# A selective-scan block with experts on one core: GpSimd takes over the copy of the scan states at the half of a row

## The chip, the cores and the metric

One core of a Trainium2 chip runs the whole program. The metric is the device time of one execution in microseconds (us). PE is TensorE, DVE is VectorE, ACT is ScalarE, POOL is GpSimd and SP is SyncE; PEld is TensorE's loading of weights.

## The reference

The input is 4 images of 32 x 32 positions with 384 channels, float32. A Mamba-like block comes first and a block of 8 experts, one for each token, second; both are added to their input. Cut to what matters here:

```
def step(h, inp):                       # selective_scan, 4 directions, 16 states n for each channel
    u_t, d_t, B_t, C_t = inp
    dA = jnp.exp(d_t[..., None] * As)
    h = h * dA + (d_t * u_t)[..., None] * B_t[:, :, None, :]
    y = jnp.einsum('bkcn,bkn->bkc', h, C_t)
    return (h, y)
...
xz = x @ in_proj_w.T; xh, z = split(xz); xc = silu(conv3x3(xh) + conv_b)
xs = [rows, columns, rows reversed, columns reversed] of xc, each 1024 positions
x_dbl = einsum(xs, x_proj_w); dts, Bs, Cs = split(x_dbl); dts = softplus(dts @ dt_projs_w + dt_projs_b)
y = sum over the 4 directions of selective_scan(...); y = layernorm(y) * silu(z); out = y @ out_proj_w.T
...
x = x + conv_block(layernorm(x)); t = x + experts(layernorm(x))      # top 1 of 8 experts
```

The recurrence over the 1024 positions is the part that the change touches. Each of the 16 states n is a scan of its own; y is the sum over n of the scan's result times C.

## The kernel before

The program handles two images at a time (a pair, `p`): the 192 channels of two images fill 3 tiles of 128 partitions (`CG = 3`). After projection, convolution and step sizes comes the scan stage, which lies at 172 to 728 us of the span for the first pair and at 971 to 1527 us for the second.

**How the scan stage is cut.** A row of 1024 positions is scanned in two halves of 512. There are 4 directions, in each of them the first half for all 16 states and then the second half for all 16 states: 8 groups of 16 steps, 128 steps for each pair. In this text a first group is one that does the first half of a direction, and a second group one that does the second half. `place(s)` gives for a step the direction, the group, the half, the state n and whether the group is a first one. A second group starts each scan from the state with which the first one ended; that is kept in `state[:, n, 0:3]`, one number for each of the 3 tiles of a partition.

**What a step is.** (1) Its input, du times B, is made by GpSimd (n = 0, 4, 8, 12), by VectorE (odd n up to 13) or by ScalarE and TensorE together (n = 2, 6, 10, 14, 15), as the letters P, D and A of `MAKER` say. (2) ScalarE makes the decay exp(delta times A), 3 instructions (`exp`, L683 into PSUM, or L678 into SBUF for the letter A), in a ring of two PSUM banks. (3) VectorE does 3 scans (`scans`, L916), in place, in one of the 7 ring slots `X3`. (4) In a first group the state is copied: column 511 of each of the 3 tiles, or column 0 where the direction runs backwards. (5) GpSimd multiplies the slot by C in place, one instruction of 128 x 1536 (L472), and counts `s_hc`. (6) TensorE adds the slot up in PSUM (`add_up`, L1203) and frees it (`s_xfree`).

**The order on each engine.** It is written out by hand. GpSimd: the input for step s + 2 where that is its own (`input_of`, L457), then waits for C and for the 3 scans of step s, in first groups also for `s_state`, then the product (L472). ScalarE: the first two exponentials of step s + 1, then `keep_state(s)` (L692), then the rest; the second of these exponentials waits for the third scan of step s. TensorE: in step s the transposes of an input of the letter A (`transpose_input`, L1229), then `add_up` of step s - 2; `transpose_du` (L1216) follows step 13. Since TensorE takes these in order, the scan of an A step s waits for the transposes, and these wait behind the add-up of step s - 3, which needs GpSimd's product of step s - 3. VectorE: the input for step s + 1 where it is its own (L892), then the 3 scans of step s. SyncE loads rows of B and C (L344), each when its ring slot is free; for C that is `s_hc`.

Of the kernel before, what the change touches and what calls it, by code (L numbers as in the profile page):

```python
# [9 lines left out]
ALU = mybir.AluOpType  # L10
ACT = mybir.ActivationFunctionType
# [7 lines left out]
CG = 3  # L19
KC = DM // P  # L20
TT = L // P
HALF = 512
# [7 lines left out]
RING, B_RING, C_RING = 7, 4, 6  # L30
# [9 lines left out]
KORDER = (0, 2, 1, 3)  # L40
# [9 lines left out]
def build(nc, x, w_in, conv_w, conv_b, w_xd, w_dt, bias_row, a_log, d_skip, ln_g, ln_b, w_out,  # L50
          w_gate, b_gate, w1, w2, w3, sel, ident_d, half_ones, tri_d, out):
    ctx = ExitStack()
    with ctx:
# [17 lines left out]
        ones = sb("ones", [P, P])  # L71
# [33 lines left out]
        X3 = [carve(CG * HALF).rearrange("p (j l) -> p j l", j=CG) for _ in range(IN_ARENA)]  # L105
# [25 lines left out]
        state = carve(NS * CG).rearrange("p (n j) -> p n j", n=NS)  # L131
# [144 lines left out]
        STEPS = ND * 2 * NS  # L276

        def place(s):

            kk, first = s // (2 * NS), (s // NS) % 2 == 0  # L280
            return kk, s // NS, int(first == (KORDER[kk] >= 2)), s % NS, first
# [8 lines left out]
        def states_before(c):  # L290
            return c // (2 * NS) * NS + min(c % (2 * NS), NS)
# [131 lines left out]
        @block.gpsimd  # L423
        def _(g):
            g.memset(padf, 0.0).then_inc(s_pad, 1)
            g.memset(ones[:, :], 1.0).then_inc(s_setup, 1)
            g.sem_inc(s_gap, 4)
            g.iota(lane[:, :], [[0, 1]], base=1, channel_multiplier=1, allow_small_or_imprecise_dtypes=True)\
             .then_inc(s_iota, 1)
            for p in range(PAIRS):  # L430
                if p:
                    g.wait_ge(s_xfree, STEPS * p)
                    g.memset(padf, 0.0).then_inc(s_pad, 1)

                for t in range(1, 9):
                    g.wait_ge(s_prod, 9 * p + t + 1)
                    if t > 1:
                        g.wait_ge(s_taps, 8 * p + t - 1)
                    g.tensor_tensor(acc3[:, BY_POOL, :], acc3[:, BY_POOL, :], tap[t % 2], ALU.add).then_inc(s_taps, 1)  # L439
                for i, kk in enumerate(PREP):  # L440
                    if i >= 2:
                        g.wait_ge(s_dust[i % 2], 16 * (2 * p + 1))
                    for j in range(CG):
                        n, d = CG * (ND * p + i) + j + 1, delta3[i % 2][:, j, :]
                        g.wait_ge(s_delta, n)
                        g.tensor_tensor(du3[i % 2][:, j, :], d, (xc3 if kk < 2 else xcT3)[:, j, :], ALU.mult)\  # L446
                         .then_inc(s_du, 1)
                def input_of(s):

                    _, gr, _, n, _ = place(s)  # L450
                    c = STEPS * p + s
                    g.wait_ge(s_steps[gr % 2], 32 * (GROUPS_OF_PAIR // 2 * p + gr // 2 + 1))
                    r = rows_before(c)
                    g.wait_ge(s_b[r % B_RING], 32 * (r // B_RING + 1))
                    if c >= RING:
                        g.wait_ge(s_xfree, c - RING + 1)
                    g.tensor_tensor(X3[c % RING], steps[gr % 2][1], Bs[r % B_RING][:, None, :].to_broadcast([P, CG, HALF]),  # L457
                                    ALU.mult).then_inc(s_dbp, 1)

                for s in range(STEPS):  # L460
                    kk, _, _, n, first = place(s)
                    c = STEPS * p + s
                    if s == 0:
                        input_of(0)
                    if s + 2 < STEPS and MAKER[(s + 2) % NS] == "P":
                        input_of(s + 2)
                    g.wait_ge(s_c[c % C_RING], 32 * (c // C_RING + 1))
                    g.wait_ge(s_scan, CG * (c + 1))
                    if first:
                        g.wait_ge(s_state, states_before(c + 1))  # L470
                    x = X3[c % RING]
                    g.tensor_tensor(x, x, Cs[c % C_RING][:, None, :].to_broadcast([P, CG, HALF]), ALU.mult)\  # L472
                     .then_inc(s_hc, 1)
                g.wait_ge(s_zld, 16 * (p + 1))
                for h in range(2):
                    cs = slice(h * HALF, (h + 1) * HALF)
                    g.wait_ge(s_yg, 2 * CG * p + CG * h + 1)
                    for b in range(2):
                        src = slice(64 * b, 64 * b + 64)
                        ins = g.tensor_tensor(yz3[0:64, b, cs], y3[src, 0, cs], g3(z2)[src, 0, cs], ALU.mult)  # L480
                    ins.then_inc(s_yzp, 1)

            g.wait_ge(s_ops, 16 * PAIRS)
            small_ok = dict(allow_small_or_imprecise_dtypes=True)
            g.iota(iota_n, [[1, NT]], base=0, channel_multiplier=0, **small_ok).then_inc(s_iota, 1)
            g.iota(rev, [[-1, NE]], base=NE, channel_multiplier=0, **small_ok).then_inc(s_iota, 1)
            g.iota(iota_m, [[1, P]], base=0, channel_multiplier=0, **small_ok).then_inc(s_iota, 1)
            g.iota(block_no, [[2 * TT, PAIRS], [1, TT], [TT, 2]], base=0, channel_multiplier=0, **small_ok)\
             .then_inc(s_iota, 1)

            g.wait_ge(s_iota, 5)
            g.wait_ge(s_tile, 1)
            g.tensor_tensor(number_of[:, :, 0, :], in_tile, block_no[:, :, None].to_broadcast([P, TILES, NT]),
                            ALU.mult).then_inc(s_num, 1)

            g.wait_ge(s_tst, 16 * 2 * GROUPS * PAIRS)
            g.wait_ge(s_first, 1)

            def load_rows(k, rows):
                g.indirect_dma_start(xs[k], None, t_dram, bass.IndirectOffsetOnAxis(rows, 0)).then_inc(s_xs[k], 16)  # L500

            for k in range(4):
                load_rows(k, first_rows[:, k:k + 1])

            def store_rows(n, k, more):

                g.wait_ge(s_gap, n + 1)
                g.wait_ge(s_yo, n + 1)
                g.tensor_tensor(gap[:, k:k + 1], one[:, :], one[:, :], ALU.mult).then_inc(s_gap, 1)  # L509

                g.indirect_dma_start(out, bass.IndirectOffsetOnAxis(move[:, k, 0:1], 0), yo[k % 2], None,
                                     bounds_check=TOK - 1, oob_is_err=False).then_inc(s_yst[k % 2], 16)
                if more:
                    load_rows(k, move[:, k, 1:2])

            with g.Fori(0, NT // 4 - 1) as i:
                for w in range(4):
                    store_rows(i * 4 + w, w, True)
            for w in range(4):
                store_rows(NT - 4 + w, w, False)  # L520
            for u in range(2):
                g.wait_ge(s_yst[u], 16 * (NT // 2))
# [3 lines left out]
        def _(a):  # L526
# [13 lines left out]
            for p in range(PAIRS):  # L540
# [142 lines left out]
                    a.activation(dA[e % 2], steps[g % 2][0][:, j, :], ACT.Exp,  # L683
                                 scale=A[:, KORDER[kk], j, n:n + 1]).then_inc(s_dA, 1)

                def keep_state(s):

                    kk, _, _, n, _ = place(s)
                    c = STEPS * p + s
                    at = 0 if KORDER[kk] >= 2 else HALF - 1  # L690
                    a.wait_ge(s_scan, CG * (c + 1))
                    a.activation(state[:, n, :], X3[c % RING][:, :, at], ACT.Copy).then_inc(s_state, 1)  # L692

                def y_out(g):

                    kk, _, half, _, _ = place(g * NS)
# [12 lines left out]
                for s in range(STEPS):  # L709
                    kk, g, _, n, first = place(s)  # L710
                    todo = [(g * NS + m if m > n else (g + 1) * NS + m, f, l) for m, f, l in SCALED.get(n, ())]
                    exp(s, 0)
                    exp(s, 1)
                    if s == 0:
                        duT_out(0)
                        du_to_psum(0)
                        scale_duT(BY_SCALAR[0], 0, 3)
                    if s and place(s - 1)[4]:
                        keep_state(s - 1)
                    if MAKER[n] == "A" or n % 2:  # L720
                        exp(s, 2)
                    if n == NS - 1 and g + 1 < GROUPS_OF_PAIR:
                        du_to_psum(g + 1)
                    for m, f, l in todo:
                        if m < STEPS:
                            scale_duT(m, f, l)
                    if n == 2 and g:
                        y_out(g - 1)
                    if not (MAKER[n] == "A" or n % 2):
                        exp(s, 2)  # L730
                    if n == NS - 2 and g + 1 < GROUPS_OF_PAIR:
                        duT_out(g + 1)
# [730 lines left out]
```

## Time and profile before

| | us |
|---|---|
| median of 3 runs | 1968.33 (1968.18 to 1974.79) |
| the profiled execution, its own time | 1967.72 |
| its span in the trace | 1965.9 |
| scan stages in it, 2 x about 555 | about 1111 |
| mean granted TensorE clock | 0.908 |

The page gives each engine's busy time over the whole span; as the stages have different limits, the scan stages are read by themselves, with views restricted to stretches of time. The waits give idle time of an engine and what ended it. The timeline gives instructions in order of time, equal neighbours merged ("x4"), with the idle time before them in brackets.

### The profile page before, as it was taken

The page shows a single profiled execution, that of the slowest core. Times are in us where ns is not written, and L with a number is a line of the kernel's source. Part 1 is how long each engine was busy: PE and PEld are TensorE (multiplying, and loading weights), DVE is VectorE, ACT ScalarE, POOL GpSimd, SP SyncE. Part 2 cuts the span into 40 slices and gives each one's busy share as a digit, 9 for nine tenths or more (in the row PEclk, how much of TensorE's full clock was granted, in tenths as well). Part 3 has the DMA queues.
Part 4 walks back from the last instruction along what each step waited for, and adds up shares of the span by engine and source line. Part 5 has one row for each costly group of instructions (what it writes and reads, how often), then busy time and mean ns, then how long its engine had stood idle before and what let it go on. Part 6 is the DMA issues. An engine that isn't in the chain of part 4 may idle for free.

```text
span 1965.9 us, 17747 instructions
## 1 busy us (share of the span) xinstructions
PE 1569.6 (80%) x5004; PEld 781.3 (40%) x5005; DVE 1467.5 (75%) x1586; ACT 1073.5 (55%) x1944; POOL 1306.9 (66%) x501
## 2 busy tenths in 40 slices
PE   5765788788888875977488878877888668999997
PEld 2222334334433432622134433433443244555554
DVE  5468999999999977455799999999999572332222
ACT  3557767777777752364677777876776211111110
POOL 1337999999999981042599999999999112222221
PEclk9876999999999997787599899999998878999999
DMA  3147345344434331212834434433432481111110
GB/s 115 43 174 247 102 130 177 97 134 149 128 105 139 102 120 67 73 38 91 310 104 138 149 112 139 134 107 130 136 100 70 181 310 38 45 48 45 51 49 14
DMA packets 107360, 228.15 MB, mean 116 GB/s; under 512 B 18302, under 2 KB 31137, under 8 KB 103440
## 3 DMA queue, kind: packets, MB, share of 16 engines
q1 hardware_dynamic: 102160, 213.02, 32.7%
q0 software_dynamic: 5120, 14.21, 2.3%
q8 instruction: 33, 0.54, 0.1%
q14 instruction: 47, 0.39, 0.1%
HBM read 184.13 MB, written 44.60 MB: 116 GB/s over the span
## 4 chain that ended last, share of the span: by engine, by line
PE 44%; DVE 21%; POOL 18%; issue 12%; ACT 4%; DMA 1%; DVEq 0%; POOLq 0%; SPq 0%; ACTq 0%
POOL arena L472 15%; DVE arena L916 13%; PE psum L1203 11%; PE psum L1341 10%; PE psum L1360 5%; PE psum L1136 3%; PE psum L1152 3%; POOL arena L457 2%; DVE arena L892 2%; PE psum L1229 2%; PE psum L1177 2%; PE psum L1269 1%; PE psum L1216 1%; PE psum L1288 1%; DVE arena L872 1%
## 5 line engine op out<-in xcount | busy, mean ns | idle before, releaser
L472 POOL TENSOR_TENSOR arena<-arena 128x1536 f32<-128x1536 f32 x256 | 877.6, 3449 | 30.9 <-ACT arena L692 16.9
L1203 PE MATMUL psum<-arena,ident 128*128 128x512 f32 x1536 | 717.7, 619 | 70.6 <-POOL arena L472 70.4
L916 DVE TENSOR_TENSOR_SCAN arena<-psum,arena 128x512 f32<-128x512 f32 x528 | 614.6, 1228 | 0.1
L683 ACT ACTIVATE psum<-arena 128x512 f32<-128x512 f32 x528 | 363.4, 690 | 259.4 <-DVE arena L916 249.3
L1203 PEld LDWEIGHTS psum<-arena,ident 128*128 128x128 f32 x1536 | 295.7, 199 | 457.0 <-issue 325.9
L916 DVE TENSOR_TENSOR_SCAN arena<-arena,psum 128x512 f32<-128x512 f32 x240 | 282.5, 1231 | 37.2 <-PE psum L1229 34.0
L1229 PE MATMUL psum<-ident,arena 128*128 128x128 f32 x960 | 154.4, 295 | 143.0 <-DVE arena L916 142.8
L660 ACT ACTIVATE arena<-arena 128x192 f32<-128x192 f32 x640 | 234.6, 440 | 0.0
L457 POOL TENSOR_TENSOR arena<-arena 128x1536 f32<-128x1536 f32 x64 | 220.4, 3443 | 0.0
L892 DVE TENSOR_TENSOR arena<-psum,arena 128x1536 f32<-128x1536 f32 x112 | 193.8, 1731 | 13.6 <-ACT psum L668 12.2
L1341 PE MATMUL psum<-arena 128*128 x480 | 203.7, 561 | 0.0
L1229 PEld LDWEIGHTS psum<-ident,arena 128*128 128x128 f32 x960 | 112.2, 148 | 201.8 <-DVE arena L916 140.5
L768 ACT ACTIVATE arena<-psum 128x384 f32<-128x384 f32 x40 | 19.6, 490 | 301.6 <-PE psum L1332 301.6
L678 ACT ACTIVATE arena<-arena 128x512 f32<-128x512 f32 x240 | 161.3, 710 | 14.2 <-DVE arena L916 14.1
L446 POOL TENSOR_TENSOR arena<-arena 128x1024 f32<-128x1024 f32 x24 | 60.4, 2517 | 148.1 <-DVE arena L877 148.1
L509 POOL TENSOR_TENSOR gap<-one 128x1 f32<-128x1 f32 x40 | 11.3, 284 | 211.9 <-DVE arena L1078 211.9
L1341 PEld LDWEIGHTS psum<-arena 128*128 128x128 f32 x480 | 88.8, 192 | 77.5 <-issue 67.3
L1061 DVE TENSOR_TENSOR arena<-arena,psum 128x469 f32<-128x469 f32 x40 | 25.7, 643 | 124.1 <-ACT arena L773 114.4
L439 POOL TENSOR_TENSOR arena<-arena 128x1024 f32<-128x1024 f32 x16 | 38.0, 2374 | 114.2 <-ACT arena L572 112.2
L1360 PE MATMUL psum<-arena 128*128 (+1 forms) x320 | 110.0, 487 | 1.0 <-DVE arena L1068 1.0
L1177 PE MATMUL psum<-arena 64*128 64x512 f32 x96 | 63.3, 807 | 24.4 <-DVE arena L877 22.6
L872 DVE SCALAR_TENSOR_TENSOR arena<-arena 128x1024 f32<-128x1024 f32 x24 | 43.5, 1811 | 51.7 <-ACT arena L624 51.6
(161 smaller groups left out, 1480.3 us busy)
## 6 DMA issues: line engine op xcount, KB each, us to landing
arena<-bc_dram SPq DMA_DIRECT2D x864, 128.0 KB, 3.0
step_dram<-arena SPq DMA_DIRECT2D x16, 1536.0 KB, 7.9
arena<-step_dram SPq DMA_DIRECT2D x32, 768.0 KB, 7.7
arena<-in_x SPq DMA_DIRECT2D x8, 1536.0 KB, 10.3
arena<-in_w SPq DMA_DIRECT2D x6, 1876.0 KB, 11.1
t_dram<-arena SPq DMA_DIRECT2D x16, 386.0 KB, 4.4
arena<-in_w SPq DMA_DIRECT2D x4, 1536.0 KB, 14.9
z_dram<-arena SPq DMA_DIRECT2D x2, 1536.0 KB, 5.1
```

Source lines behind the costliest of these rows:

```text
L457: g.tensor_tensor(X3[c % RING], steps[gr % 2][1], Bs[r % B_RING][:, None, :].to_broadcast([P, CG, HALF]), ALU.mult).then_inc(s_dbp, 1)
L472: g.tensor_tensor(x, x, Cs[c % C_RING][:, None, :].to_broadcast([P, CG, HALF]), ALU.mult)\
L660: a.activation(blocks(scaled[index % 2])[:, :, k, b, :], blocks(duT)[:, :, k, b, :], ACT.Copy, scale=BT[:, kk, LB * half + k, b, BY_SCALAR ...
L678: a.activation(dAs[j], steps[g % 2][0][:, j, :], ACT.Exp, scale=A[:, KORDER[kk], j, n:n + 1]).then_inc(s_dAs, 1)
L683: a.activation(dA[e % 2], steps[g % 2][0][:, j, :], ACT.Exp, scale=A[:, KORDER[kk], j, n:n + 1]).then_inc(s_dA, 1)
L892: v.tensor_tensor(X3[c % RING], dups, Bs[r % B_RING][:, None, :].to_broadcast([P, CG, HALF]), ALU.mult).then_inc(s_dbv, 1)
L916: v.tensor_tensor_scan(x, decay, given, 0.0 if first else state[:, n, j:j + 1], ALU.mult, ALU.add).then_inc(s_scan, 1)
L1177: ins = pe.matmul(bank[2 + 2 * j + h], wdt[0:64, KORDER[PREP[i]], j, :], xd[i % 2][0:64, h * HALF:(h + 1) * HALF], start=True, stop=True)
L1203: ins = pe.matmul(bank[j], ident[:, :], X3[c % RING][:, j, :], start=False, stop=(n == NS - 1), skip_group_check=True)
L1229: ins = pe.transpose(dA[e % 2][:, k * P:(k + 1) * P], scaled[index % 2][:, at:at + P], ident[:, :])
L1341: ins = pe.matmul(bk[:, 0:F], xsT[u][:, k, :], w[:, k, bass.ds(e * F, F)], start=(k == 0), stop=(k == KC - 1))
L1360: ins = pe.matmul(bank[6 + u][:, 0:DM], hidT[u][0:m, k, :], W3[0:m, k, bass.ds(e * DM, DM)], start=(k == 0), stop=(k == FC - 1))
```

## The change

In a first group GpSimd copies the state itself, ahead of its product with C; the copy is a multiplication of 128 x 3 numbers (stride 512) by ones. The wait for `s_state`, which was for ScalarE's copy, now is for its own copy. ScalarE's `keep_state`, and its wait for the scans, are gone. There are 16 such copies in each of 4 first groups for 2 pairs, 128 in all.

```diff
@@ -466,9 +466,11 @@
                         input_of(s + 2)
                     g.wait_ge(s_c[c % C_RING], 32 * (c // C_RING + 1))
                     g.wait_ge(s_scan, CG * (c + 1))
+                    x = X3[c % RING]
                     if first:
+                        at = 0 if KORDER[kk] >= 2 else HALF - 1
+                        g.tensor_tensor(state[:, n, :], x[:, :, at], ones[:, 0:CG], ALU.mult).then_inc(s_state, 1)
                         g.wait_ge(s_state, states_before(c + 1))
-                    x = X3[c % RING]
                     g.tensor_tensor(x, x, Cs[c % C_RING][:, None, :].to_broadcast([P, CG, HALF]), ALU.mult)\
                      .then_inc(s_hc, 1)
                 g.wait_ge(s_zld, 16 * (p + 1))
@@ -683,14 +685,6 @@
                     a.activation(dA[e % 2], steps[g % 2][0][:, j, :], ACT.Exp,
                                  scale=A[:, KORDER[kk], j, n:n + 1]).then_inc(s_dA, 1)
 
-                def keep_state(s):
-
-                    kk, _, _, n, _ = place(s)
-                    c = STEPS * p + s
-                    at = 0 if KORDER[kk] >= 2 else HALF - 1
-                    a.wait_ge(s_scan, CG * (c + 1))
-                    a.activation(state[:, n, :], X3[c % RING][:, :, at], ACT.Copy).then_inc(s_state, 1)
-
                 def y_out(g):
 
                     kk, _, half, _, _ = place(g * NS)
@@ -715,8 +709,6 @@
                         duT_out(0)
                         du_to_psum(0)
                         scale_duT(BY_SCALAR[0], 0, 3)
-                    if s and place(s - 1)[4]:
-                        keep_state(s - 1)
                     if MAKER[n] == "A" or n % 2:
                         exp(s, 2)
                     if n == NS - 1 and g + 1 < GROUPS_OF_PAIR:
```

## Rows read from the trace of the kernel before

**Rows 1.** The page, part 1: busy time, share of the span and instructions of each engine.
```profile
PE 1569.6 (80%) x5004; PEld 781.3 (40%) x5005; DVE 1467.5 (75%) x1586; ACT 1073.5 (55%) x1944; POOL 1306.9 (66%) x501
```

**Rows 2.** Two groups: stretch, PE, PEld, DVE, ACT, POOL busy, PEclk, DMA share, GB/s.
```profile
172.50:241.10 68.60, 50.26 (x158) 25.24 (x159) 65.32 (x56) 50.23 (x106) 64.12 (x19) 0.90 0.34 112
241.10:310.80 69.70, 57.22 (x173) 27.75 (x172) 68.46 (x57) 50.79 (x94) 68.48 (x21) 0.95 0.39 125
```

**Rows 3.** Timeline of POOL, first direction and first group of the second.
```profile
176.92 6.84 POOL L472 TENSOR_TENSOR arena<-arena 128x1536 f32<-128x1536 f32 x2 [6.43 <-ACT arena L692]
...
187.11 13.65 POOL L472 TENSOR_TENSOR arena<-arena 128x1536 f32<-128x1536 f32 x4
200.71 3.44 POOL L457 TENSOR_TENSOR arena<-arena 128x1536 f32<-128x1536 f32 x1
204.11 13.74 POOL L472 TENSOR_TENSOR arena<-arena 128x1536 f32<-128x1536 f32 x4
...
221.20 13.63 POOL L472 TENSOR_TENSOR arena<-arena 128x1536 f32<-128x1536 f32 x4
...
262.32 6.97 POOL L472 TENSOR_TENSOR arena<-arena 128x1536 f32<-128x1536 f32 x2 [0.25 <-DVE arena L916]
...
315.25 6.88 POOL L472 TENSOR_TENSOR arena<-arena 128x1536 f32<-128x1536 f32 x2 [0.70 <-ACT arena L692]
...
350.18 6.86 POOL L472 TENSOR_TENSOR arena<-arena 128x1536 f32<-128x1536 f32 x2 [0.82 <-ACT arena L692]
```

**Rows 4.** Timeline of all engines, the turn from first to second group.
```profile
223.24 6.78 DVE L916 TENSOR_TENSOR_SCAN arena<-psum,arena 128x512 f32<-128x512 f32 x6
...
228.07 2.84 PE L1203 MATMUL psum<-arena,ident 128*128 128x512 f32 x6 [0.55 <-POOL arena L472]
...
232.06 1.04 PE L1229 MATMUL psum<-ident,arena 128*128 128x128 f32 x8
...
232.80 6.78 DVE L916 TENSOR_TENSOR_SCAN arena<-arena,psum 128x512 f32<-128x512 f32 x6 [2.78 <-PE psum L1229]
```

**Rows 5.** Timeline of DVE, second group of the first direction.
```profile
241.14 7.15 DVE L916 TENSOR_TENSOR_SCAN arena<-psum,arena 128x512 f32<-128x512 f32 x6
...
258.56 7.15 DVE L916 TENSOR_TENSOR_SCAN arena<-psum,arena 128x512 f32<-128x512 f32 x6
...
301.88 7.35 DVE L916 TENSOR_TENSOR_SCAN arena<-arena,psum 128x512 f32<-128x512 f32 x6 [1.13 <-PE psum L1229]
```

**Rows 6.** Waits of POOL, whole span: us in total, times, longest us.
```profile
POOL arena L472 <- ACT arena L692: 16.9, 11, 6.4
POOL arena L472 <- DVE arena L916: 10.8, 30, 0.5
```

**Rows 7.** Waits of DVE in the scans, and of PE for POOL, whole span.
```profile
DVE arena L916 <- PE psum L1229: 34.0, 25, 3.6
DVE arena L916 <- ACT arena L678: 1.9, 2, 1.0
PE psum L1203 <- POOL arena L472: 70.4, 56, 3.1
```

**Rows 8.** Timeline of ACT at the start of the second direction; groups by line for L692.
```profile
314.27 0.69 ACT L683 ACTIVATE psum<-arena 128x512 f32<-128x512 f32 x1 [0.42 <-DVE arena L916]
314.89 0.19 ACT L692 ACTIVATE arena<-arena 128x3 f32<-128x3 f32 x1
...
L692 ACT ACTIVATE arena<-arena 128x3 f32<-128x3 f32 x128 | 24.9, 195 | 9.8 <-DVE arena L916 9.8
```

**Rows 9.** Instructions of a line on POOL: duration ns min/median/max; the smallest one by group.
```profile
L509 POOL TENSOR_TENSOR gap<-one x40: 183/287/323, 1645.2 to 1956.0; 128x1 f32<-128x1 f32 x40
L446 POOL TENSOR_TENSOR arena<-arena x24: 2345/2352/3412, 83.9 to 963.2; 128x1024 f32<-128x1024 f32 x24
L472 POOL TENSOR_TENSOR arena<-arena x256: 3417/3448/3479, 176.9 to 1523.5; 128x1536 f32<-128x1536 f32 x128
L439 POOL TENSOR_TENSOR arena<-arena x16: 2351/2380/2385, 43.7 to 858.1; 128x1024 f32<-128x1024 f32 x16
L428 POOL IOTA lane<- 128x1 f32 x1 | 0.1, 127 | 0.0
```

**Rows 10.** Timeline of POOL: eight dependent sums (L439), and the expert stage.
```profile
43.71 20.01 POOL L439 TENSOR_TENSOR arena<-arena 128x1024 f32<-128x1024 f32 x8 [39.67 <-ACT arena L572]
...
1677.73 0.28 POOL L509 TENSOR_TENSOR gap<-one 128x1 f32<-128x1 f32 x1 [5.11 <-DVE arena L1078]
1678.50 1.02 POOL L511 DMA_INDIRECT out<-arena,move  x1 [0.48 <-issue]
```

## The prediction, made before the changed kernel ran

> **What bounds the kernel now.** The busy shares of the page come first, and they mislead: GpSimd is at 66% and VectorE at 75% of the whole span [rows 1]. The change lies in the scan stages alone, so I read those by themselves. Over one direction VectorE is busy for 65.3 of 68.6 us in the first group and 68.5 of 69.7 us in the second; GpSimd for 64.1 us of the first (it can't begin before the first scan is done, at 176.9) and 68.5 us of the second [rows 2]. Both are nearly full, so the question is which of them waits for the other, and where.
>
> GpSimd's timeline answers that. It starts at 176.92 and then runs without a pause through the whole first group; the first idle time is the 0.25 us at 262.32, in the second group. Later first groups have few pauses, the longest of them 0.82 us at 350.18 [rows 3]. Four steps of a first group hold 4 products and one input, 5 instructions of 128 x 1536, and start again after 204.11 - 187.11 = 17.0 us, so one instruction takes a pitch of 3.40 us (less than its recorded 3.448 us [rows 9], since neighbours overlap a little). VectorE's pace in a first group would be 6.78 us for six scans. That VectorE is the faster one there shows at its step 14: it ends its scans at 223.24 + 6.78 = 230.0 and stands still for 2.78 us [rows 4]. What ends that stall, TensorE's transposes of the input, stands in TensorE's order behind the add-up of step 11, and that began at 228.07, when GpSimd's product was done [rows 4]. So in first groups **GpSimd sets the pace**, through TensorE's queue; VectorE waits 34.0 us for these transposes in all, and TensorE 70.4 us for GpSimd [rows 7].
>
> In a second group the six scans take 7.15 us, and four steps 258.56 - 241.14 = 17.42 us [rows 5]. There VectorE is the slower one, by 0.42 us in four steps; GpSimd waits for it in small pieces, 0.25 us at 262.32 for one [rows 3]. Still step 14 of the second group stalls for 1.13 us on the transposes [rows 5], so even there GpSimd is right behind.
>
> How much does GpSimd stand still? The two waits of L472 add up to 16.9 + 10.8 = 27.7 us [rows 6]. Two of them, 6.43 us for the first pair and as much for the second, are the start of a pair, when there is no scan to multiply yet. What is left is 27.7 - 12.9 = 14.8 us in the 8 directions, under 2 us in each. That is all the slack of the engine that gets the new work.
>
> **The change part by part.** (a) *ScalarE loses 128 copies* of 195 ns, 24.9 us busy [rows 8]. ScalarE's exponentials hold up no scan: among VectorE's waits in the scans only 1.9 us is for ScalarE [rows 7], and ScalarE is busy for 50 of 69 us of a group [rows 2]. I take this at nothing; the upper bound of the gain is the 1.9 us.
>
> (b) *GpSimd no longer waits for ScalarE.* This wait can be seen where GpSimd has caught up: at the start of the second direction ScalarE first does an exponential (314.27, 0.69 us), then the copy (314.89, 0.19 us), and GpSimd's product starts at 315.25 [rows 3, 8]. The copy could have started about 0.1 us after the scan, at about 314.3, but GpSimd itself was busy until 314.55. At each pair's start some 0.9 us of the 6.43 us is of this kind (0.69 + 0.19), nearly 2 us for both pairs. In the steps at which GpSimd lags behind, the copy was long done, and nothing is saved.
>
> (c) *GpSimd gets 128 copies, and each is followed by a wait for itself.* The trace has no 128 x 3 product on GpSimd. The nearest row is the 128 x 1 product L509, 287 ns (183 to 323) [rows 9]. A line through 1024 elements in 2.352 us and 1536 in 3.448 us has a slope of 2.14 ns an element and meets zero elements at 0.16 us, so 3 elements would take 0.17 us. The smallest instruction of any kind took 0.127 us [rows 9]. I take 0.25 us, between the line and the 128 x 1 row and nearer to the latter. The wait for its own semaphore also has a row: the eight L439, each of which waits for the one before, cover 20.01 us, with 2.38 us each; 20.01 - 2.38 = 17.63 us for 7 pitches is 2.52 us, so 0.14 us pass between the end of one and the start of the next [rows 9, 10]. Copy and wait: 0.25 + 0.14, about **0.40 us for each**, with bounds of 0.127 + 0.14 = 0.27 us and, from above, 0.77 us, the time from the start of L509 to the start of the instruction behind it (1677.73 to 1678.50), which is an indirect DMA with an issue of its own [rows 10]. Something like 0.6 us is the highest that I give weight. Queued behind the waiting copy on GpSimd are the product of the same step and the input of step s + 4; who waits for them is TensorE's add-up, then VectorE at the next A step, and SyncE with the C row, whose slot is 6 steps deep and hides it.
>
> The Trainium skill bears on this (Perfetto Trace Analysis, GPSIMD Engine Instruction): it says that recorded spans of GpSimd don't compose and that starts should be compared with starts. By recorded span alone a copy is 0.28 us and the sum would be 128 x 0.28 - 15 = +21 us; by the one start-to-start figure there is, 0.77 us, it would be +84 us. The L439 rows agree with the rule: 2.38 us recorded, 2.52 us from start to start.
>
> (d) *What takes up the new work.* 128 x 0.40 = 51 us go onto an engine that is the bound in every first group. Nothing hides a copy there: in the first direction GpSimd has no idle time from its first product to the fifth of the second group. What comes off is the slack. A GpSimd that enters the second group later doesn't meet its small waits for VectorE any more, and waits less at the next direction's start: at most the 14.8 us. In the last group of a pair no new direction follows and VectorE sets the pace to the end, so I take only about 13 us of them. With the 2 us of (b) that is **15 us saved**, bounds 11 and 18 us. The second bound holds if neighbours of a small wait become quicker too (two products took 6.97 us behind such a wait and 6.84 us without [rows 3]).
>
> (e) *Beyond GpSimd.* From the end of product 11 to the start of scan 14 there are 4.7 us (228.07 to 232.80 [rows 4]), three scans take 3.4 us more; GpSimd has three instructions, 10.2 us, and two copies to do before it needs that scan. So the way over TensorE gives GpSimd no new wait, and TensorE's clock, 0.90 and 0.95 in these groups [rows 2], has over 2 us of room.
>
> Sum: 1967.7 + 51 - 15 = 2003.7; the median lies 0.6 us above the profiled execution, so **2004 us**.
>
> **The rivals.** *One, VectorE is the bound and the copies are hidden.* For it: 75% against 66% busy, and GpSimd does wait 30 times for scans. Then the time stays within some 5 us of 1968. Against it: the 2.78 and 1.13 us stalls of VectorE, both behind GpSimd, and a first group in which GpSimd never stands still [rows 3]. *Two, the other side: the removed wait is worth more than the copy.* The point from which it decides is 15 / 128 = 0.12 us for a copy with its wait. If GpSimd took the copy in 0.05 us, the sum would be 6.4 - 15 = -9 us, 1959 us. For it: where GpSimd caught up, it saves an exponential and a copy on ScalarE. Against it: the own wait alone measured 0.14 us. *Three, a dear copy.* A small instruction between two large ones costs what it costs ahead of the DMA, near 0.7 us: 128 x 0.7 - 13 = +77 us, 2045 us. For it: the only start-to-start figure of a small product. Against it: 0.48 us of that stand as issue of the indirect DMA. *Four, a cheap one.* Copy and wait at the lower bounds, 0.27 us: 35 - 17 = +18 us, 1986 us.
>
> **How the numbers follow.** Forecast, 0.32 to 0.5 us for each copy, 1992 to 2019 us: 0.60. Cheap copy, 1979 to 1992: 0.13. Dear, above 2019: 0.16, most of it under 2045. VectorE the bound: 0.08. Gain: 0.03. The range reaches from the cheap copy to 0.6 us for each with 12 us saved (77 - 12 = +65 us): 1984 to 2033. About 0.5%, 10 us, is what a measurement of this kernel can tell from no change. Slower by more: 0.60 + 0.16 + 0.13 less a little of the cheap case, 0.88. Within: 0.09. Faster: 0.03.
>
> **What would show it.** Right: GpSimd's waits in the scans fall from 27.7 us to the start of each pair and little more; the first step of L472 after a copy starts 0.4 us after the copy's start; VectorE's waits for the transposes grow from 34 us to some 70 us and more; each direction takes 4 to 5 us longer, nearly all of it in its first group; nothing changes outside the scan stages. Wrong: GpSimd keeps idle time in second groups, or first groups grow by less than 16 copies; or the copy's start-to-start time isn't near 0.4 us, which scales the sum and nothing else.

## The result: slower by 1.2%, and where the time went

| | us |
|---|---|
| before, median of 4 runs beside it | 1971.34 (1968.18 to 1974.79) |
| changed, median of 4 runs | 1995.69 (1994.41 to 1996.58) |
| ratio | 1.0123, 95% interval 1.0099 to 1.0146 |
| profiled execution: before, changed | 1967.72, 1995.23 |
| its span: before, changed | 1965.9, 1993.4 |

The lines move by 2 to 8: GpSimd's product is L474 now and its copy L472, the scans are L908, the transposes L1221, the add-up L1195. The waits of GpSimd in the changed kernel answer [rows 6]:

```profile
POOL arena L472 <- DVE arena L908: 11.1, 2, 5.6
POOL arena L474 <- DVE arena L908: 6.9, 20, 0.6
```

No wait for ScalarE is left; 27.7 us have become 18.0 us, 11.1 us of them at the two starts of a pair. The waits of VectorE and TensorE answer [rows 7]:

```profile
DVE arena L908 <- PE psum L1221: 60.1, 31, 5.5
PE psum L1195 <- POOL arena L474: 91.1, 55, 4.0
```

VectorE stands still for 60.1 us before its scans and not 34.0, TensorE waits 91.1 us for GpSimd's product and not 70.4. The start of GpSimd's timeline answers [rows 3]:

```profile
176.86 0.19 POOL L472 TENSOR_TENSOR arena<-arena,ones 128x3 f32<-128x3 f32 x1 [5.56 <-DVE arena L908]
177.14 3.44 POOL L474 TENSOR_TENSOR arena<-arena 128x1536 f32<-128x1536 f32 x1
180.53 0.19 POOL L472 TENSOR_TENSOR arena<-arena,ones 128x3 f32<-128x3 f32 x1
180.81 3.44 POOL L474 TENSOR_TENSOR arena<-arena 128x1536 f32<-128x1536 f32 x1
184.20 3.43 POOL L457 TENSOR_TENSOR arena<-arena 128x1536 f32<-128x1536 f32 x1
...
283.50 6.97 POOL L474 TENSOR_TENSOR arena<-arena 128x1536 f32<-128x1536 f32 x2 [0.24 <-DVE arena L908]
```

From the copy's start to the product's start 0.28 us pass, and the product still ends 3.39 us after its start as far as the next instruction is concerned. Nothing overlaps the copy. In this first direction there is no idle time up to 283.50, the ninth product of the second group. At step 14 of the first group, where VectorE stood still for 2.78 us [rows 4], it now stands still for 4.86 us:

```profile
224.91 6.79 DVE L908 TENSOR_TENSOR_SCAN arena<-psum,arena 128x512 f32<-128x512 f32 x6
236.55 6.78 DVE L908 TENSOR_TENSOR_SCAN arena<-arena,psum 128x512 f32<-128x512 f32 x6 [4.86 <-PE psum L1221]
```

**Where the time lies.** VectorE begins each group with an input of its own (L892, now L884), so the starts of these instructions cut the span into groups. In the profiled execution of before the 8 first groups add up to 554.4 us, of the changed kernel to 578.5 us: +24.1 us, 3.0 us for each. The six second groups that have a successor take 417.0 and 416.3 us. The stretch ahead of the first group is 0.8 us longer, the one from the last group of the first pair to the second pair 0.4 us shorter, and all from the last group on 3.7 us longer. 24.1 - 0.7 + 0.8 - 0.4 + 3.7 = 27.5 us, the difference of the two spans. VectorE's instructions didn't get slower: it is busy for 1467.5 us before and 1467.4 us now.

Where one group is taken to end matters a little. Counted on GpSimd, from its first product of a group to its first product of the next, the first groups grow from 549.0 to 579.0 us (30.0 of the 35.5 us that 128 copies of 0.277 us add), and the six second groups shrink from 421.0 to 416.5 us. The table below uses VectorE's count; where GpSimd's says something else, the text gives it.

The 3.7 us at the end lie in the stage between the scans and the experts. The same stretch, from 80 us behind the start of the last group to 332 us before the end, is in before and in the changed kernel (busy time of PE, PEld, DVE, ACT, POOL, then the granted clock):

```profile
1534.60:1633.90 99.30, 60.11 (x281) 37.02 (x282) 64.15 (x138) 22.31 (x36) 16.90 (x13) 0.74 0.59 220
1558.38:1661.40 103.02, 65.55 (x281) 39.57 (x282) 64.38 (x138) 20.89 (x35) 16.90 (x13) 0.70 0.57 212
```

The same 281 matmuls take 60.1 us of TensorE at a mean granted clock of 0.74 and 65.6 us at 0.70. Of the kernels below, e2 and e3 show 0.74 and 0.73 there, e1 and e4 0.69, with no link to the edit that I can see.

### The profile page after: what moved, and what is told of

Read it like the earlier page. It is cut to its first block, busy times and chain, and to the rows that moved or that the text cites. A ratio compares the mean times of both kernels' runs of the same rounds, so it can differ in the third digit from the quotient of the medians.

```text
span 1993.4 us, 17747 instructions
## 1 busy us (share of the span) xinstructions
PE 1583.2 (79%) x5004; PEld 785.6 (39%) x5005; DVE 1467.4 (74%) x1586; ACT 1061.0 (53%) x1816; POOL 1331.1 (67%) x629
## 4 chain that ended last, share of the span: by engine, by line
PE 42%; POOL 20%; DVE 19%; issue 14%; ACT 3%; DMA 1%; DVEq 0%; POOLq 0%; ACTq 0%
POOL arena L474 16%; PE psum L1195 12%; DVE arena L908 10%; PE psum L1333 10%; PE psum L1352 5%; PE psum L1144 3%; POOL arena L457 2%; PE psum L1128 2%; PE psum L1221 2%; PE psum L1169 2%; DVE arena L884 1%; DVE arena L864 1%; POOL arena L439 1%; PE psum L1208 1%; PE psum L1343 1%
## 5 line engine op out<-in xcount | busy, mean ns | idle before, releaser
L474 POOL TENSOR_TENSOR arena<-arena 128x1536 f32<-128x1536 f32 x256 | 880.4, 3450 | 18.8 <-DVE arena L908 6.9
L1195 PE MATMUL psum<-arena,ident 128*128 128x512 f32 x1536 | 729.3, 627 | 91.6 <-POOL arena L474 91.1
L908 DVE TENSOR_TENSOR_SCAN arena<-psum,arena 128x512 f32<-128x512 f32 x528 | 615.1, 1233 | 0.1
L1195 PEld LDWEIGHTS psum<-arena,ident 128*128 128x128 f32 x1536 | 299.3, 201 | 485.8 <-issue 330.9
L908 DVE TENSOR_TENSOR_SCAN arena<-arena,psum 128x512 f32<-128x512 f32 x240 | 281.8, 1233 | 61.1 <-PE psum L1221 60.1
L1221 PE MATMUL psum<-ident,arena 128*128 128x128 f32 x960 | 150.2, 291 | 133.2 <-DVE arena L908 133.2
L884 DVE TENSOR_TENSOR arena<-psum,arena 128x1536 f32<-128x1536 f32 x112 | 194.3, 1735 | 13.0 <-ACT psum L670 12.2
L1221 PEld LDWEIGHTS psum<-ident,arena 128*128 128x128 f32 x960 | 110.3, 145 | 189.9 <-DVE arena L908 129.1
L680 ACT ACTIVATE arena<-arena 128x512 f32<-128x512 f32 x240 | 158.4, 710 | 17.4 <-DVE arena L908 17.4
L439 POOL TENSOR_TENSOR arena<-arena 128x1024 f32<-128x1024 f32 x16 | 38.0, 2377 | 114.4 <-ACT arena L574 112.4
L1169 PE MATMUL psum<-arena 64*128 64x512 f32 x96 | 63.3, 806 | 24.4 <-DVE arena L869 22.6
## 6 DMA issues: line engine op xcount, KB each, us to landing
arena<-in_w SPq DMA_DIRECT2D x4, 1536.0 KB, 12.6
```

The costliest lines, as they stand in the source:

```text
L680: a.activation(dAs[j], steps[g % 2][0][:, j, :], ACT.Exp, scale=A[:, KORDER[kk], j, n:n + 1]).then_inc(s_dAs, 1)
L884: v.tensor_tensor(X3[c % RING], dups, Bs[r % B_RING][:, None, :].to_broadcast([P, CG, HALF]), ALU.mult).then_inc(s_dbv, 1)
L908: v.tensor_tensor_scan(x, decay, given, 0.0 if first else state[:, n, j:j + 1], ALU.mult, ALU.add).then_inc(s_scan, 1)
L1169: ins = pe.matmul(bank[2 + 2 * j + h], wdt[0:64, KORDER[PREP[i]], j, :], xd[i % 2][0:64, h * HALF:(h + 1) * HALF], start=True, stop=True)
L1195: ins = pe.matmul(bank[j], ident[:, :], X3[c % RING][:, j, :], start=False, stop=(n == NS - 1), skip_group_check=True)
L1221: ins = pe.transpose(dA[e % 2][:, k * P:(k + 1) * P], scaled[index % 2][:, at:at + P], ident[:, :])
```

## The experiments

Each kernel ran beside the kernel before on its chip. The medians of the kernel before differ by up to 5.4 us from set to set (1968.3 to 1973.7), so kernels of different sets are best compared by their ratios. The two sums are those of above, from one profiled execution of each kernel: 8 first groups, and 6 second groups. The diffs leave out new tiles and semaphores.

| kernel | median us | ratio to before (95%) | first groups | second groups |
|---|---|---|---|---|
| before | 1968 to 1974 | 1 | 554.4 | 417.0 |
| changed | 1995.69 | 1.0123 (1.0099 to 1.0146) | 578.5 | 416.3 |
| e1 copy twice | 2024.38 | 1.0253 (1.0236 to 1.0270) | 602.2 | 421.3 |
| e2 both copies | 1991.77 | 1.0087 (1.0070 to 1.0104) | 581.8 | 416.4 |
| e3 shorter product | 1958.40 | 0.9917 (0.9900 to 0.9933) | 548.0 | 415.9 |
| e4 ScalarE earlier | 1969.91 | 0.9982 (0.9964 to 1.0001) | 551.4 | 417.9 |
| f1 copy by VectorE | 2039.94 | 1.0344 (1.0317 to 1.0372) | 625.6 | 417.0 |
| f2 bare product | 1990.34 | 1.0093 (1.0066 to 1.0120) | 572.5 | 416.6 |
| f3 copies in second groups | 1995.03 | 1.0117 (1.0088 to 1.0146) | 558.2 | 434.4 |
| f4 an input to VectorE | 1978.92 | 1.0032 (1.0012 to 1.0051) | 562.0 | 422.0 |
| h1 reduction by VectorE | 1976.82 | 1.0022 (1.0003 to 1.0040) | 568.7 | 416.3 |
| h2 changed + f4 | 1985.30 | 1.0063 (1.0041 to 1.0085) | 564.1 | 421.9 |
| h3 e4 + f4 | 1969.14 | 0.9981 (0.9960 to 1.0002) | 551.3 | 422.6 |

**e1, each copy twice.**

```diff
                     if first:
                         at = 0 if KORDER[kk] >= 2 else HALF - 1
+                        g.tensor_tensor(state[:, n, :], x[:, :, at], ones[:, 0:CG], ALU.mult).then_inc(s_twice, 1)
+                        g.wait_ge(s_twice, states_before(c + 1))
                         g.tensor_tensor(state[:, n, :], x[:, :, at], ones[:, 0:CG], ALU.mult).then_inc(s_state, 1)
```

> The changed kernel with each copy done twice, each followed by its own wait (256 copies). A copy takes 0.277 us from its start to the start of the product in the trace of the changed kernel. Theory A (GpSimd's own time sets the pace of the first groups): 128 x 0.277 = 35 us more, less what is left of GpSimd's small waits for scans (6.9 us there, of which at most 5 go): +30 to +35 us over the changed kernel, about 2026 us. Theory B (the time comes from another place, such as one wait in each step that hides a second copy, or VectorE as the bound): under +10 us.

Measured 2024.4 us, +28.7 us over the changed kernel by the medians and +26 us by the ratios: 1 to 4 us under theory A's range, and far from theory B's 10 us. The first groups grew by another 23.7 us and the second ones by 5.0 us (on GpSimd's count by 30.6 and -0.8 us, so a second copy costs there what the first did). The copies stand one behind the other at 0.27 us:

```profile
176.95 0.19 POOL L473 TENSOR_TENSOR arena<-arena,ones 128x3 f32<-128x3 f32 x1 [5.55 <-DVE arena L911]
177.22 0.19 POOL L475 TENSOR_TENSOR arena<-arena,ones 128x3 f32<-128x3 f32 x1
177.49 3.44 POOL L477 TENSOR_TENSOR arena<-arena 128x1536 f32<-128x1536 f32 x1
```

The product's waits for scans shrink from 6.9 us to 1.8 us; what little slack there was is used up.

**e2, ScalarE's copy kept and GpSimd's work added.**

```diff
                     x = X3[c % RING]
+                    if first:
+                        at = 0 if KORDER[kk] >= 2 else HALF - 1
+                        g.tensor_tensor(spare[:, n, :], x[:, :, at], ones[:, 0:CG], ALU.mult).then_inc(s_extra, 1)
+                        extra[0] += 1
+                        g.wait_ge(s_extra, extra[0])
                     g.tensor_tensor(x, x, Cs...
```

> The kernel before, ScalarE's copy kept, and in first groups an extra copy of the same 128 x 3 numbers by GpSimd into a spare tile, with its own wait. It does the second half of the change (GpSimd's work) without the first (ScalarE's copy gone). Theory A: as the changed kernel, plus the 0.87 us at each of the two starts of a pair: +26 to +29 us over before, about 1997 us. Theory B (the change costs because the copy itself now lies on the way of the state): the extra copy is needed by nobody, so clearly less than the changed kernel, under +15 us.

The first groups grew by 27.4 us over before, 3.3 us more than with the change: a copy that nobody needs costs as much as the real one, so it is GpSimd's time and not the way of the state. The time as a whole is a miss: the ratio gives +17 us (14 to 20) over before where +26 to +29 us was expected, close to theory B's bound of 15 us. The kernel before took 1973.7 us beside it; against before's profiled execution, 6 us faster, e2's profiled span is 24.3 us longer. The median is also 4 us under the changed kernel's: all from the last group on took 510.9 us, the changed kernel's 515.1 us, at a granted clock of 0.74 and 0.70 in the stage behind the scans. So theory A rests here on the group sums, where the edit acts, and not on the median.

**e3, a shorter product.** The product leaves out 129 of 1536 elements in first groups.

```diff
-                    g.tensor_tensor(x, x, Cs[c % C_RING][:, None, :].to_broadcast([P, CG, HALF]), ALU.mult)\
+                    w = HALF - 43 if first else HALF
+                    g.tensor_tensor(x[:, :, 0:w], x[:, :, 0:w], Cs[c % C_RING][:, None, 0:w].to_broadcast([P, CG, w]), ALU.mult)\
```

> The changed kernel, but the product with C leaves out the last 43 of 512 columns of each tile in first groups (129 of 1536 elements), so that part of the product is left out. At 2.14 us for 1000 elements that is 0.276 us less for each product, as much as a copy with its wait takes. Theory A: GpSimd's time in a step is that of before, the time goes back to the kernel before or 2 to 6 us under it: 1963 to 1972 us. Theory B (not GpSimd's time in total but the waits around the copy): stays near 1996 us.

1958.4 us, 37 us under the changed kernel. Taking 128 x 0.28 = 36 us off GpSimd gives back all that the copies took, and more than the expected return to before: the first groups are 6.4 us under before, 0.8 us each. From start to start the shorter product takes 3.13 us where the whole one takes 3.40, so GpSimd's time in a step is that of before here, and I read the 6.4 us as what the change gains by not waiting for ScalarE. On GpSimd's count it is 3.2 us in first groups and 3.0 us in second ones. e2, which keeps ScalarE's copy, is 3.3 us over the changed kernel in first groups; e4 shows 3.0 us, not clear of noise. The time is 5 us below the expected range. Theory B is out.

**e4, ScalarE's copy one exponential earlier**, in the kernel before.

```diff
                     exp(s, 0)
+                    if s and place(s - 1)[4]:
+                        keep_state(s - 1)
                     exp(s, 1)
...
-                    if s and place(s - 1)[4]:
-                        keep_state(s - 1)
```

> The kernel before, with ScalarE's copy of the state put between its first and second exponential of the next step, so that it runs when the third scan is done and not one exponential (0.69 us) later. Theory A: only GpSimd's waits for ScalarE shrink, which are 16.9 us in 11 places, 11 of them unavoidable at the two starts of a pair: 0.5 to 0.7 us at most of them, -3 to -6 us against before, 1963 to 1968 us. Rival (the later exponential delays the scans, which wait for it): +5 us or more.

The ratio of 0.9982 (0.9964 to 1.0001) fits -3 to -6 us but isn't clear of no change; the first groups are 3.0 us shorter, the second ones 0.9 us longer, and on GpSimd's count the two sums together are those of before (969.8 and 970.0 us). So a gain isn't shown. The rival, +5 us, is out.

**f1, the copy by VectorE**, behind its scans, with a wait for them; GpSimd's copy is gone.

```diff
                     scans(s)
+                    kk, _, _, n, first = place(s)
+                    if first:
+                        ...
+                        v.wait_ge(s_scan, CG * (c + 1))
+                        v.tensor_copy(state[:, n, :], X3[c % RING][:, :, at]).then_inc(s_state, 1)
```

> The changed kernel with the copy given to VectorE, right behind the three scans of the step and after a wait for them; GpSimd waits for it as it did for ScalarE. Theory A (GpSimd sets the pace of first groups, VectorE has 34 us of waits for TensorE there): VectorE's extra 128 x some 0.2 to 0.3 us go into its own waits, and GpSimd's wait for a state shrinks by some 0.5 us where it has caught up: 0 to -5 us against before. Rival (VectorE is the bound in first groups): 128 x 0.25 = +30 us against before, as much as the change itself.

A clear miss: +69 us, and the first groups 71.2 us longer. VectorE's timeline shows why, with GpSimd's beside it:

```profile
185.77 1.22 DVE L906 TENSOR_TENSOR_SCAN arena<-arena,psum 128x512 f32<-128x512 f32 x1 [0.17 <-PE psum L1225]
187.03 1.70 DVE L918 COPY arena<-arena 128x3 f32<-128x3 f32 x1
188.64 3.44 DVE L906 TENSOR_TENSOR_SCAN arena<-psum,arena 128x512 f32<-128x512 f32 x3
...
226.03 2.07 DVE L918 COPY arena<-arena 128x3 f32<-128x3 f32 x1
```

```profile
185.28 3.42 POOL L457 TENSOR_TENSOR arena<-arena 128x1536 f32<-128x1536 f32 x1
...
224.65 3.43 POOL L457 TENSOR_TENSOR arena<-arena 128x1536 f32<-128x1536 f32 x1
```

The copy of 3 numbers that begins at 187.03 lasts until 188.73; GpSimd's product that was running ends at 188.70. The one at 226.03 ends at 228.10, GpSimd's at 228.08. All copies show it: the 26 that begin while GpSimd is idle take 0.168 to 0.171 us, and each of the 102 that begin while it works ends 0.02 to 0.03 us after GpSimd's running instruction. The 128 copies last 0.168 to 3.43 us, 734 ns in the mean, 93.9 us in all; that is 72 us over 128 x 0.17 us, and the first groups grew by 71.2 us. A copy of VectorE waits until GpSimd's running instruction is through, and the scans behind it wait as well. It is neither theory's mechanism; h1 tests it.

**f2, a small product without its wait**, in first groups of the kernel before.

```diff
+                    if first:
+                        m = states_before(c)
+                        g.tensor_tensor(spare[:, m, :], ones[:, 0:CG], ones[:, CG:2 * CG], ALU.mult)
```

> The kernel before, ScalarE's copy kept, and in first groups an extra product of 128 x 3 ones on GpSimd into a spare tile of its own, with no wait behind it. It measures what a small instruction costs on GpSimd without the wait for itself. In the changed kernel 0.277 us pass from the copy's start to the product's start, 0.199 us of it the recorded copy. Theory A1 (the cost is mostly the instruction): 0.15 to 0.2 us for each from start to start, first groups 8 x 16 x 0.17 - 6 = +12 to +20 us longer than before. A2 (the cost is mostly the wait, small instructions overlap as the start-up fills do at 0.03 us): under +5 us.

```profile
182.38 0.20 POOL L475 TENSOR_TENSOR spare<-ones 128x3 f32<-128x3 f32 x1
182.52 3.43 POOL L476 TENSOR_TENSOR arena<-arena 128x1536 f32<-128x1536 f32 x1
```

0.15 us from start to start (127 of the 128), at a recorded 0.195 us, and the first groups grew by 18.1 us: A1 holds. So of the 0.28 us of the change about 0.15 us are the small instruction and 0.13 us the wait for it. The change itself without that wait wasn't tried: the product overwrites in place what the copy reads, and only the wait orders the two.

**f3, the extra copies of e2 in second groups only** (`if not first`).

> The kernel before with the extra GpSimd copy and its own wait (0.277 us) in second groups only, 128 of them. Theory A with slack: in second groups VectorE is the slower by 0.42 us in four steps and GpSimd waits 1 to 2 us in each; so of 4.4 us for each group 1.5 to 2 us are hidden: +19 to +24 us over before, a little less than in first groups. Rival (VectorE alone sets the pace there): under +8 us.

+23 us by the ratio, and 434.4 - 417.0 = 17.4 us in six second groups, 2.9 us each, of the 16 x 0.28 = 4.4 us that were added; the first groups grew by 3.8 us. Second groups, whose pace VectorE sets by a hair, pay nearly as much as first ones (3.4 us in e2). The slack there is 1.5 us, as expected, and no more.

**f4, one input from GpSimd to VectorE**, in the kernel before; the string has 32 letters now, for a first and a second group, and is indexed by the step modulo 32.

```diff
-MAKER = "PDADPDADPDADPDAA"
+MAKER = "PDADPDADPDADDDAAPDADPDADPDADPDAA"
```

> The kernel before (ScalarE's copy), but in first groups VectorE, not GpSimd, makes the input of n = 12: 3.4 us off GpSimd and 1.65 us onto VectorE in each of 8 first groups. Theory A: VectorE's stall of 2.8 us at step 14 of a first group goes, 1.65 us of it is refilled: -1 to -1.7 us for each first group, -8 to -14 us against before, second groups unchanged. Rival (VectorE is the bound): +13 us.

A miss again: 1978.9 us, 6 us slower than before by the ratio (2 to 10), with first groups 7.6 us longer in sum where I expected 8 to 14 us less. First and second groups together are 12.6 us longer (on either count), nearly the rival's +13 us: VectorE's added time, 8 x 1.65 us, came through almost whole. The 2.78 us stall did shrink to 0.89 us, but GpSimd, with 3.4 us less to do, now stands still before three products in a row:

```profile
220.05 3.44 POOL L472 TENSOR_TENSOR arena<-arena 128x1536 f32<-128x1536 f32 x1 [1.49 <-ACT arena L692]
225.06 3.44 POOL L472 TENSOR_TENSOR arena<-arena 128x1536 f32<-128x1536 f32 x1 [1.57 <-ACT arena L692]
230.06 6.87 POOL L472 TENSOR_TENSOR arena<-arena 128x1536 f32<-128x1536 f32 x2 [1.57 <-ACT arena L692]
```

Its steps last 3.35 + 1.65 = 5.0 us, VectorE's time for three scans and an input. So GpSimd is ahead as the bound by very little: take some work off it and put it on VectorE, and VectorE with the way over ScalarE's copy is the bound at once. The waits for that copy are 64.5 us in 36 places, against 16.9 us in 11.

**h1, the state by a reduction of VectorE** in place of f1's copy.

```diff
-                        v.tensor_copy(state[:, n, :], X3[c % RING][:, :, at]).then_inc(s_state, 1)
+                        v.tensor_reduce(state[:, n, :], X3[c % RING][:, :, at:at + 1], AX_X, ALU.max).then_inc(s_state, 1)
```

> VectorE keeps the state as in f1_vector_copy, but by a reduction (maximum over one element) instead of a copy. In f1 the copies lasted 0.168 to 3.43 us, and the long ones ended when a product of GpSimd ended. Theory C (the copy takes a port that GpSimd's running instruction holds, and the reduction, which reads one input in the plain mode, does not): no long ones, some 0.2 us a step on VectorE, first groups at 68.5 to 69.5 us as before: 1968 to 1978 us. Rival (the wait for its own scan, or any small read of VectorE, is what costs): as f1, 2030 to 2040 us.

```profile
L918 DVE TENSOR_REDUCE arena<-arena x128: 156/158/160, 177.8 to 1469.4; 128x3 f32<-128x3 f32 x128
```

All 128 take 156 to 160 ns, beside f1's 168 to 3430 ns for the same numbers (min, median and max):

```profile
L918 DVE COPY arena<-arena x128: 168/250/3430, 177.9 to 1523.7; 128x3 f32<-128x3 f32 x128
```

The time falls from 2039.9 to 1976.8 us. The first groups, 71.1 us each, miss the expected 68.5 to 69.5 us; the profiled execution took 1987.6 us, 11 us more than the median, and how much of this lies in the groups isn't known. Only the kind of instruction differs from f1, so it is the copy's wait for GpSimd that costs 63 us, and theory C holds in its effect. The Trainium skill (GPSIMD Engine Reference, Key points) says that GpSimd shares its interfaces to SBUF with VectorE and conflicts with VectorE's instructions in a two-port mode or with two SBUF inputs. The two runs agree with a conflict of this kind: 0.158 us for each reduction, up to 3.43 us for a copy. No row names the mode of either instruction, so that the mode is the reason isn't shown.

**h2, the changed kernel with f4's edit.**

> The changed kernel, with the input of n = 12 in first groups made by VectorE instead of GpSimd. Theory A (GpSimd's own time bounds the first groups of the changed kernel: 20 instructions at 3.40 us and 16 copies at 0.277 us = 72.4 us, measured 71.6 to 73.5): 3.4 us come off GpSimd, and VectorE (65.2 + 1.65 us and some stalls) takes over at 68.5 to 69.5 us, -2.5 to -3.5 us for each first group: -20 to -28 us against the changed kernel, 1968 to 1976 us. Rival (something else than GpSimd's time, as the latency of copy and wait): +0 to -8 us against it.

The right sign, half the size: -10 us by the medians, -14.4 us in the first groups (1.8 us each, expected 2.5 to 3.5), +5.6 us in the second ones. The first group of the first direction falls from 71.6 to 68.7 us, the others by 0.6 to 3.0 us. So GpSimd's time was the bound of the changed kernel, but of the 3.4 us taken off it in each direction only 1.1 us came through (-14.4 + 5.6 us in 8 directions): the next bound lies 1 to 3 us lower. The growth of the second groups in f4, h2 and h3 (5.0, 4.9 and 5.6 us over before) depends on the count: in f4 their stall at step 14 is 2.42 us where it was 1.13 [rows 5], but counted on GpSimd the second groups are 419.6, 414.8 and 413.2 us, under before's 421.0, and the growth lies in the first ones (563.0, 575.5 and 562.2 us against 549.0).

**h3, f4 and e4 together.**

> f4_input_to_vector (input of n = 12 by VectorE) together with e4_scalar_copy_earlier. In f4 GpSimd waited 64.5 us for ScalarE's copies, 36 times, since a GpSimd with less to do runs right behind VectorE and meets ScalarE's exponential (0.69 us) ahead of the copy. With the copy ahead of that exponential these waits shrink by 0.7 us each: about -3 us to -8 us against f4, 1971 to 1976 us. If it falls to 1960 us the version beats both kernels; if it stays at f4's 1979 us, ScalarE's latency was not what held f4.

1969.1 us, 9.8 us under f4, a bit more than expected, all of it in first groups (562.0 to 551.3 us). So ScalarE's exponential ahead of the copy did hold f4, though GpSimd's waits for the copies only fell from 64.5 to 57.6 us; VectorE's for the transposes fell from 31.2 to 20.1 us. Against before the ratio is 0.9981 (0.9960 to 1.0002): no version here that does the whole work beats the kernel before clearly.

## Why the prediction was right, and which terms were off

The forecast was 2004 us in 1984 to 2033 us; 1995.7 us came. The mechanism with the most chance (GpSimd sets the pace of first groups, nothing hides a copy) is the one that happened. The time lies in that case's 1992 to 2019 us, but its price didn't hold: 0.277 us for a copy is rival four's 0.27, which by its own sum gave 1986 us. That 1995.7 came and not 1986 is due to 5 us less of savings than that sum took (12, not 17) and 4 us outside the scans, and that is luck as far as the prediction goes. So is some of the closeness in level: as a growth, 36 us was forecast, and the runs side by side show 24.4 us, the profiled spans 27.5 us. The kernel before took 1971.3 us beside the changed one, 3.0 us more than in the runs that the forecast started from.

**What bounds the kernel** was right. In the first groups the growth follows GpSimd's added time whatever it is spent on: -6.4 us with none added (e3), +18.1 us for 0.15 us each (f2), +27.4 us for a copy that nobody needs (e2), +24.1 us for the change, +47.8 us for two copies (e1). The rival that VectorE is the bound and hides the copies is out; f3, with 17.4 us for copies in second groups alone, says that even there little hides. So is the gain: a copy would have to cost under 0.12 us with its wait, and 0.28 was measured. What I said too strongly is how far GpSimd leads as the bound: h2 shows the next one 1 to 3 us below, and in f4, with less on GpSimd and more on VectorE, the time went up.

**Part (a), ScalarE's copies at nothing:** ScalarE's busy time fell from 1073.5 to 1061.0 us, and VectorE's 1.9 us of waits for it in the scans are gone. Right.

**Part (b), the wait for ScalarE:** at a pair's start the idle time fell from 6.43 to 5.56 us, 0.87 us as worked out. What the whole wait was worth can be read from first groups, as 6.4 us by e3 and 3.3 us by e2. The prediction took 2 us here and counted the rest in the slack of part (d).

**Part (c) is the term that was mis-sized**: 0.28 us for each copy with its wait, not 0.40 us. The record:

```profile
L472 POOL TENSOR_TENSOR arena<-arena,ones x128: 185/198/223, 176.9 to 1479.7; 128x3 f32<-128x3 f32 x128
```

The copy is 0.198 us and not 0.25: I leaned to the 128 x 1 product of the expert stage (0.287 us), which follows an idle time of 5.3 us in the mean, when the line through the two large sizes gave 0.17. The gap to the product is 0.08 us and not the 0.14 us of the dependent sums L439, which also wait for ScalarE's product. This term was 128 x 0.12 = 15 us too high; 12 us taken up in place of 15, and 4 us outside the scans, went the other way, which leaves the miss of 8 us.

**Part (d), 15 us saved:** 128 x 0.28 = 35.5 us were added, the scan groups grew by 24.1 - 0.7 = 23.4 us, so 12 us were taken up, within the bounds of 11 to 18. The way is as told: on GpSimd's count the second groups give back 4.5 us. With a cheaper copy GpSimd enters the second group less late, so it still meets VectorE there: 6.9 us of small waits stay, and I had said "little more" than the pair's start. Each direction grew by 3 us, not 4 to 5, and VectorE's wait for the transposes to 60 us and not to "70 us and more"; both are scaled by part (c). That the growth lies in first groups was right. Two things that the prediction named as signs of being wrong did come in a weak form: GpSimd keeps idle time in second groups (the 6.9 us), and first groups grow by less than 16 copies (3.0 us on VectorE's count and 3.75 on GpSimd's, where 16 x 0.277 = 4.4). The added work is hidden a little more than "nothing hides a copy" says, and e1, e2 and f2 still show it to be the cause.

**Part (e), no new wait over TensorE:** GpSimd has no idle time at product 14 of the first group in the changed kernel's timeline. Right. "Nothing changes outside the scan stages" was wrong by about 4 us: the stage behind the scans ran at a granted clock of 0.70 and not 0.74.

Beside the rule of the Trainium skill (Perfetto Trace Analysis, GPSIMD Engine Instruction): starts compared with starts in the changed kernel give 0.28 us, and 0.15 us in f2 where no wait follows, both unlike the recorded 0.20 us, so these traces agree with the rule. The 0.77 us that I had by it ran up to an indirect DMA, an instruction of another kind; no small product measured here costs as much.

## What to carry to other kernels

Read the stage in which the edit acts: GpSimd was at 66% and VectorE at 75% of the span, and yet a small instruction in each step of GpSimd came through at two thirds of its price. Count a moved instruction by its start-to-start time plus the wait for its own semaphore, which here cost as much again. When two engines are within 1 to 3 us in 70 of each other, neither adding to one nor relieving one works as the sum for that engine alone says.

## What the runs showed of the hardware

- A small product on GpSimd (128 x 3) between large ones: 0.195 us recorded, 0.15 us from start to start (f2, 127 of 128 places), 0.28 us with a wait for its own semaphore behind it (changed kernel, 0.26 to 0.30 us at all 128 places).
- A VectorE copy of 128 x 3 float32 from SBUF to SBUF waits for the GpSimd instruction that is running, up to 3.43 us, in 102 of 102 cases, and takes 0.17 us when GpSimd is idle (f1, 26 cases); a reduction of the same numbers takes 0.158 us each time (h1). This was worth 63 us in the kernel.
- The stretch between the scans and the experts takes 99 us at a mean granted TensorE clock of 0.74 and 103 us at 0.70 for the same instructions. The kernel before itself spread from 1963.8 to 1980.6 us on one chip. Its fastest run there had a mean granted clock of 0.912, its slowest 0.897, and over the 13 runs time and clock go together (correlation -0.81; -0.76 and -0.80 in the two other sets); which of the two drives the other no run shows.
